# The router's sum: one-hots over nodes made by transposition instead of by comparison

## The chip, the core and the metric

The program runs on one core of one Trainium2 chip. The metric is the device time of one execution in microseconds (us), the median of several. A core has TensorE (PE; its weight loads are shown apart as PEld), VectorE (DVE), ScalarE (ACT), GpSimd (POOL) and SyncE (SP, which here only issues transfers). Each works through its own instructions in order; semaphores tie them together. L1985 means line 1985 of the kernel.

## What is computed

A graph block over 6250 nodes with 256 features: a graph transformer with two layers over 200,000 edges, a linear attention beside it, and a mixture of four experts, whose gates come from a graph attention router over 131,072 other edges. The change is in the router. Cut to that:

```python
h = (x_flat @ W_gat).reshape(M, HEADS, NUM_EXPERTS)      # 4 heads, 4 experts
src = concatenate([edge_index[0], loops]); dst = concatenate([edge_index[1], loops])
a_src = (h * att_src).sum(-1); a_dst = (h * att_dst).sum(-1)
e = leaky_relu(a_src[src] + a_dst[dst], 0.2)
e_max = segment_max(e, dst, num_segments=M)
ee = exp(e - e_max[dst])
denom = segment_sum(ee, dst, num_segments=M)
alpha = ee / (denom[dst] + 1e-16)
agg = segment_sum(h[src] * alpha[:, :, None], dst, num_segments=M)
```

## The kernel before

The program is a row of blocks, one after the other, with a barrier between: two edge lists are sorted by node tile, the two attention layers run over the first list, then the router over the second: `neighbour_max` (the maximum per node, with the experts beside it), `router_weights`, `neighbour_sum`, `gates`, and `answer`, which adds the experts' outputs to the result.

The change is in `neighbour_sum` alone. Nodes lie in 50 tiles of 125 (`NODE_TILE`). The sorted edges come in tiles of 128 lanes, two edge tiles (a pair) always belonging to one node tile. A step handles `WIDE` = 8 edge tiles, so 4 pairs; there are 141 steps, and all code is written out (`edge_steps`): in loop step n each engine runs its pieces in the order of its list, piece with lag l on edge step k = n + l. Buffers are picked by k modulo 2 or 4, and semaphores count steps.

Per step:

- SyncE (L1950) loads, for all partitions alike, the place of each of the 1024 edges in its node tile (`local`, 256 KB).
- VectorE, `near_hot` (L2060): compares `local` with the partition's number and gets `hot_t`, 125 nodes by 1024 edges, bf16, zeros and ones.
- TensorE, `fetch` (L2004): eight small matmuls with `hot_t` as weights take, for each edge, its destination's numbers from `node_info`; which tile is in a register, read eight at a time in every second step by `load_tiles` (L666, `TENSOR_LOAD`).
- VectorE, `gather_info` (L2049): sums the three bf16 parts into `info`.
- GpSimd, VectorE, ScalarE: `sums` (L1980), `leaky` (L2065), `less` (L1985), `exps` (L2027), `weigh` (L1963), and the split of the result into three bf16 parts: `high` (L2032), `rest_of` (L1970), `middle` (L2036), `low` (L1975).
- VectorE, `one_hot` (L2054): compares the numbers 0 to 124 (`node_no`, copied once to 8 x 125) with each edge's place (`g.loc`) and gets `hot`, 128 edges by 8 x 125 nodes, bf16. It holds the same ones as `hot_t`, the other way round.
- TensorE, `add_up` (L2015): eight matmuls with `hot` as weights sum the parts of the edges per node, two edge tiles into one piece of PSUM.
- VectorE, `add_sum(0..3)` (L2078): four additions of such a piece to `acc3` at the tile that a register tells. Each waits for the previous one, since two may meet the same tile.

The orders on the engines before:

```python
steps(pool, [(0, sums), (-1, less), (-2, weigh), (-3, rest_of), (-4, low)])
steps(pe, [(1, load_tiles), (-5, add_up), (1, fetch)])
steps(act, [(-3, high), (-4, middle), (-1, exps)])
steps(dve, [(0, gather_info), (-6, add_sum(0)), (-1, leaky), (-6, add_sum(1)), (2, near_hot), (-6, add_sum(2)),
            (-2, one_hot), (-6, add_sum(3)), (-6, load_tiles)])
```

Of the kernel before, what the change touches and what calls it, by code (L numbers as in the profile page):

```python
# [7 lines left out]
ALU = mybir.AluOpType  # L8
# [4 lines left out]
BF16 = mybir.dt.bfloat16  # L13
# [3 lines left out]
LANES = 128  # L17
PAIR = 2
NODE_TILE = 125
# [59 lines left out]
@contextmanager  # L79
def semaphores(nc, names):  # L80

    handles = [nc.alloc_semaphore(name=n) for n in names]
    yield handles
    nc.clear_and_free_semaphores(handles)
    nc.all_engine_barrier()


def sem_set(nc, ctx, prefix, names):
    handles = ctx.enter_context(semaphores(nc, [f"{prefix}_{n}" for n in names]))
    return dict(zip(names, handles))  # L90
# [491 lines left out]
def at(tensor, t):  # L582

    return tensor[:, t] if isinstance(t, int) else tensor[:, bass.ds(t, 1)].squeeze(1)
# [12 lines left out]
def wait(eng, sem, value):  # L597

    if not isinstance(value, int) or value > 0:
        eng.wait_ge(sem, value)  # L600
# [1304 lines left out]


WIDE = 8
SPLIT_SUMS = SPLIT * (FE + FH)


def neighbour_sum(nc, c, g, src_sb, node_info, gacc, ans):

    pairs = WIDE // PAIR
    with ExitStack() as st:
        def sb(n, shape, dt=F32):
            return st.enter_context(nc.sbuf_tensor(f"gs_{n}", shape, dt))

        def psum(n):
            return [st.enter_context(nc.psum_tensor(f"gs_{n}{h}", [LANES, 512], F32)) for h in range(2)]

        node_no = sb("node_no", [LANES, WIDE, NODE_TILE], BF16)
        hot = sb("hot", [LANES, 4, WIDE, NODE_TILE], BF16)
        local = sb("local", [LANES, 4, WIDE * LANES], BF16)
        hot_t = sb("hot_t", [NODE_TILE, 2, WIDE * LANES], BF16)
        info = sb("info", [LANES, 4, WIDE, 2 * FH])
        e_sb = sb("e_sb", [LANES, 4, WIDE, FH])
        vals = sb("vals", [LANES, 4, WIDE, FE + FH])
        rest = sb("rest", [LANES, 4, WIDE, FE + FH])
        parts = sb("parts", [LANES, 4, WIDE, SPLIT, FE + FH], BF16)
        acc3 = sb("acc3", [NODE_TILE, g.tiles, SPLIT_SUMS])  # L1930
        tile_of = sb("tile_of", [1, g.pairs], I32)
        ps_n, ps_sum = psum("ps_n"), psum("ps_sum")
        m = sem_set(nc, st, "gs", ["tiles_in", "cleared", "one_hots", "near_hots", "fetched", "info", "sums", "leaky",
                                   "less", "exps", "weighted", "high", "rest", "middle", "split", "summed", "added",
                                   "chain"])
        m["local_in"] = st.enter_context(semaphores(nc, [f"gs_local_in{j}" for j in range(4)]))
# [3 lines left out]
        def steps(eng, pieces):  # L1940
            edge_steps(eng, total, pieces)
# [47 lines left out]
        @block.tensor  # L1989
        def _(pe):  # L1990
            pe.wait_ge(m["tiles_in"], 16)

            numbers = TileNumbers(nc, pe, tile_of, g)

            def load_tiles(k, r, j):
                numbers.load((k + 1) * pairs)

            def fetch(k, r, j):
                pe.wait_ge(m["near_hots"], k + 1)
                wait(pe, m["info"], k - 1)  # L2000
                for p in range(pairs):
                    t = numbers.of(k * pairs + p)
                    for e in range(PAIR * p, PAIR * (p + 1)):
                        ins = pe.matmul(ps_n[j % 2][:, e * SPLIT * 2 * FH:(e + 1) * SPLIT * 2 * FH],  # L2004
                                        hot_t[:, j % 2, e * LANES:(e + 1) * LANES],
                                        at(node_info, t).rearrange("p n f -> p (n f)"), start=True, stop=True)
                ins.then_inc(m["fetched"], 1)

            def add_up(k, r, j):
                pe.wait_ge(m["split"], k + 1)  # L2010
                pe.wait_ge(m["one_hots"], k + 1)
                wait(pe, m["added"], pairs * (k - 2) + pairs)
                for p in range(pairs):
                    for e in range(PAIR):
                        ins = pe.matmul(ps_sum[j % 2][0:NODE_TILE, p * SPLIT_SUMS:(p + 1) * SPLIT_SUMS],  # L2015
                                        hot[:, k % 4, PAIR * p + e, :],
                                        parts[:, k % 4, PAIR * p + e].rearrange("p n f -> p (n f)"),
                                        start=e == 0, stop=e == PAIR - 1)
                ins.then_inc(m["summed"], 1)
            steps(pe, [(1, load_tiles), (-5, add_up), (1, fetch)])  # L2020

        @block.scalar
        def _(act):
            def exps(k, r, j):
                act.wait_ge(m["less"], k + 1)
                wait(act, m["split"], (k - 4) + 1)
                act.activation(vals[:, k % 4, :, FE:FE + FH], e_sb[:, k % 4], ACT.Exp).then_inc(m["exps"], 1)  # L2027

            def high(k, r, j):
                act.wait_ge(m["weighted"], k + 1)  # L2030
                wait(act, m["summed"], (k - 4) + 1)
                act.copy(parts[:, k % 4, :, 0, :], vals[:, k % 4]).then_inc(m["high"], 1)  # L2032

            def middle(k, r, j):
                act.wait_ge(m["rest"], k + 1)
                act.copy(parts[:, k % 4, :, 1, :], rest[:, k % 4]).then_inc(m["middle"], 1)  # L2036
            steps(act, [(-3, high), (-4, middle), (-1, exps)])

        @block.vector
        def _(dve):  # L2040
            chain = Chain(dve, m["chain"])
            dve.memset(acc3[:], 0.0)
            chain(dve.tensor_copy(node_no[:], c.node_no[:, 0:1, :].broadcast_to([LANES, WIDE, NODE_TILE])))
            dve.wait_ge(m["tiles_in"], 16)

            def gather_info(k, r, j):
                dve.wait_ge(m["fetched"], k + 1)
                wait(dve, m["less"], (k - 4) + 1)
                dve.tensor_reduce(info[:, k % 4], ps_n[j % 2][:, 0:WIDE * SPLIT * 2 * FH]  # L2049
                                  .rearrange("p (e n f) -> p e f n", e=WIDE, n=SPLIT), AX, ALU.add).then_inc(m["info"], 1)  # L2050

            def one_hot(k, r, j):
                wait(dve, m["summed"], (k - 4) + 1)
                dve.tensor_tensor(hot[:, k % 4], node_no[:], g.loc[:, bass.ds(k * WIDE, WIDE)].unsqueeze(2)  # L2054
                                  .broadcast_to([LANES, WIDE, NODE_TILE]), ALU.is_equal).then_inc(m["one_hots"], 1)

            def near_hot(k, r, j):
                dve.wait_ge(m["local_in"][j], (r + 1) * 16)
                wait(dve, m["fetched"], k - 1)
                dve.tensor_scalar(hot_t[:, j % 2, :], local[0:NODE_TILE, j], c.lane_no[0:NODE_TILE, :], None, ALU.is_equal)\  # L2060
                    .then_inc(m["near_hots"], 1)

            def leaky(k, r, j):
                dve.wait_ge(m["sums"], k + 1)
                dve.scalar_tensor_tensor(out=e_sb[:, k % 4], in0=e_sb[:, k % 4], scalar=0.2, in1=e_sb[:, k % 4],  # L2065
                                         op0=ALU.mult, op1=ALU.max).then_inc(m["leaky"], 1)

            numbers = TileNumbers(nc, dve, tile_of, g)

            def load_tiles(k, r, j):  # L2070
                numbers.load((k + 1) * pairs)

            def add_sum(p):
                def add(k, r, j):
                    t = numbers.of(k * pairs + p)
                    dve.wait_ge(m["summed"], k + 1)
                    wait(dve, m["added"], pairs * k + p)
                    dve.tensor_tensor(at(acc3, t), at(acc3, t), ps_sum[j % 2][0:NODE_TILE, p * SPLIT_SUMS:  # L2078
                                                                              (p + 1) * SPLIT_SUMS], ALU.add)\
                        .then_inc(m["added"], 1)  # L2080
                return add
            steps(dve, [(0, gather_info), (-6, add_sum(0)), (-1, leaky), (-6, add_sum(1)), (2, near_hot), (-6, add_sum(2)),
                        (-2, one_hot), (-6, add_sum(3)), (-6, load_tiles)])
            dve.wait_ge(m["added"], pairs * total)
            for n in range(SPLIT):
                chain(dve.tensor_tensor(gacc[:], gacc[:], acc3[:, :, n * (FE + FH):(n + 1) * (FE + FH)], ALU.add))
# [358 lines left out]
```

## Time and profile before

| what | value |
|---|---|
| median of 3 runs | 7925.82 us (7924.39 to 7932.85) |
| profiled execution | 7930.16 us, its span 7927.9 us |
| `neighbour_sum`, first L2060 to last L2078 | 7363.4 to 7781.3 us |
| L2054, one-hots over nodes | 141 of them, median 1187 ns |
| L2060, one-hots over edges | 141, median 637 ns |
| L2015 and L2004, matmuls | 1128 each |
| L2078, additions | 564, median 204 ns |
| after the router's sum: `gates` and `answer` | to 7927.9 us |

The span is that of the instructions the profiler saw, the execution's time includes a little around it. In a timeline a row is one instruction, or several alike that follow each other (xN); durations of neighbours on one engine may overlap, since the next one starts before the last is written, so the start-to-start distance tells what a piece costs its engine. Brackets at a row's end tell how long the engine stood idle and who released it.

### The profile page before, as it was taken

The page shows a single profiled execution, that of the slowest core. Times are in us where ns is not written, and L with a number is a line of the kernel's source. Part 1 is how long each engine was busy: PE and PEld are TensorE (multiplying, and loading weights), DVE is VectorE, ACT ScalarE, POOL GpSimd, SP SyncE. Part 2 cuts the span into 40 slices and gives each one's busy share as a digit, 9 for nine tenths or more (in the row PEclk, how much of TensorE's full clock was granted, in tenths as well). Part 3 has the DMA queues.
Part 4 walks back from the last instruction along what each step waited for, and adds up shares of the span by engine and source line. Part 5 has one row for each costly group of instructions (what it writes and reads, how often), then busy time and mean ns, then how long its engine had stood idle before and what let it go on. Part 6 is the DMA issues. An engine that isn't in the chain of part 4 may idle for free. (4 is left out here: it accounts for less than half of the span.)

```text
span 7927.9 us, 103405 instructions
## 1 busy us (share of the span) xinstructions
PE 5293.5 (67%) x27325; PEld 4204.5 (53%) x27325; DVE 5852.9 (74%) x15897; ACT 1022.4 (13%) x3273; POOL 5163.2 (65%) x5420
## 2 busy tenths in 40 slices
PE   5886855665665566556666666666559999999441
PEld 3553534555555555535555555555546666666331
DVE  7878845666666666667787878877766777777997
ACT  0000010000000000020000000000132222222230
POOL 2331306777777777737777777777617777777892
PEclk7555578778778877877887778878758888888555
DMA  1000034444444444434444444444432333332336
GB/s 31 3 3 8 3 95 125 129 128 129 128 129 128 128 129 130 128 97 126 126 127 126 125 125 126 126 125 126 125 82 52 63 62 57 62 63 55 114 96 179
DMA packets 504010, 776.97 MB, mean 98 GB/s; under 512 B 121545, under 2 KB 364222, under 8 KB 503442
## 3 DMA queue, kind: packets, MB, share of 16 engines
q0 software_dynamic: 202656, 454.22, 21.7%
q1 hardware_dynamic: 292838, 304.95, 14.7%
q10 hardware_dynamic: 7948, 11.21, 0.6%
q8 instruction: 237, 3.88, 0.2%
q14 instruction: 331, 2.71, 0.1%
HBM read 698.60 MB, written 71.36 MB: 97 GB/s over the span
## 5 line engine op out<-in xcount | busy, mean ns | idle before, releaser
L700 POOL DMA_INDIRECT att_kv_e<-kv,gnn_idx x3336 | 3366.1, 1009 | 1196.5 <-issue 1004.8
L773 PE MATMUL att_ps_sum<-att_vals,att_hot 128*125 128x136 f32 x6672 | 1345.1, 361 | 1638.6 <-DVE att_vals L822 1637.8
L773 PEld LDWEIGHTS att_ps_sum<-att_vals,att_hot 128*125 128x125 f32 x6672 | 1131.4, 246 | 1852.8 <-DVE att_vals L822 1845.7
L700 POOL DMA_INDIRECT max_rows<-rows,gat_idx x1128 | 1064.8, 944 | 568.3 <-issue 329.0
L798 DVE TENSOR_TENSOR att_prod<-att_ps_q,att_kv_e 128x512 f32<-128x512 f32 x834 | 575.9, 690 | 999.6 <-DMA att_kv_e<-kv,gnn_idx 633.5
L761 PE MATMUL att_ps_q<-qs,att_hot_t 125*128 x6672 | 1217.8, 344 | 26.9 <-DVE att_hot_t L811 26.9
L761 PEld LDWEIGHTS att_ps_q<-qs,att_hot_t 125*128 125x128 f32 x6672 | 1167.1, 262 | 28.1 <-issue 28.1
L1854 DVE CUSTOM_DVE_ANT_0 max_junk<-max_far,max_ps_b 125x256 bf16<-125x256 bf16 x2256 | 792.5, 416 | 259.2 <-PE max_ps_b L1818 256.1
L784 ACT ACTIVATE att_vals<-att_clipped 128x32 f32<-128x32 f32 x834 | 191.3, 229 | 4049.9 <-DVE att_clipped L830 4049.9
L838 DVE TENSOR_TENSOR acc<-acc,att_ps_sum 125x136 f32 x1668 | 484.4, 290 | 123.1 <-PE att_ps_sum L773 2.8
L822 DVE TENSOR_TENSOR att_vals<-att_kv_e,att_vals 128x512 f32<-128x512 f32 x834 | 567.6, 681 | 0.0
L817 DVE TENSOR_REDUCE att_dots<-att_prod 128x32 f32<-128x512 f32 x834 | 564.6, 677 | 0.1
L804 DVE TENSOR_TENSOR att_hot<-node_no,gnn_loc 128x500 f32<-128x500 f32 x834 | 558.4, 670 | 0.0
L2253 PE MATMUL ex_ps_o<-ex_w,ex_hid 128*125 128x256 f32 x1600 | 518.6, 480 | 0.0
L811 DVE TENSOR_SCALAR att_hot_t<-att_local,lane_no 125x512 f32<-125x512 bf16 x834 | 406.4, 487 | 42.3 <-DMA att_local<-gnn_loc_rows 42.3
L509 POOL DMA_INDIRECT gnn_table<-gnn_records,gnn_dest_sb x120 | 174.3, 1452 | 401.7 <-DVE gnn_records L425 372.2
L1818 PE MATMUL max_ps_b<-max_a_t,pick_head 12*125 12x512 bf16 x1128 | 375.6, 434 | 64.5 <-ACT max_a_t L1827 51.8
L2264 PE MATMUL ex_ps_h<-ex_xT,ex_w 128*128 128x250 f32 x1600 | 413.5, 404 | 0.0
L2253 PEld LDWEIGHTS ex_ps_o<-ex_w,ex_hid 128*125 128x125 f32 x1600 | 356.0, 234 | 89.4 <-issue 14.0
L480 PE MATMUL gnn_ps_perm<-gnn_moves,gnn_hot_low 125*128 125x96 f16 x1600 | 327.9, 387 | 81.6 <-DVE gnn_moves L430 81.6
L2264 PEld LDWEIGHTS ex_ps_h<-ex_xT,ex_w 128*128 128x128 f32 x1600 | 342.7, 214 | 57.9 <-issue 0.4
L480 PEld LDWEIGHTS gnn_ps_perm<-gnn_moves,gnn_hot_low 125*128 125x128 f16 x1600 | 235.2, 150 | 188.5 <-DVE gnn_moves L430 113.1
(445 smaller groups left out, 6887.5 us busy)
## 6 DMA issues: line engine op xcount, KB each, us to landing
att_local<-gnn_loc_rows SPq DMA_DIRECT2D x834, 128.0 KB
att_kv_e<-kv,gnn_idx POOLq DMA_INDIRECT x3336, 3.0
max_local<-gat_loc_rows SPq DMA_DIRECT2D x282, 128.0 KB
gs_local<-gat_loc_rows SPq DMA_DIRECT2D x141, 256.0 KB, 3.3
outs<-ex_y SPq DMA_DIRECT2D x25, 896.0 KB
max_rows<-rows,gat_idx POOLq DMA_INDIRECT x1128
ans_late<-outs SPq DMA_DIRECT2D x11, 896.0 KB
ans_early<-outs SPq DMA_DIRECT2D x8, 896.0 KB
```

The costliest lines, as they stand in the source:

```text
L480: ins = pe.matmul(ps_perm[k % 2][:, 0:2 * SLOTS_F], hot_low[:, k % 2, :, w], moves[:, k % 2, :, :, w], start=w == 0, stop=w == BLOCK - 1)
L700: pool.indirect_dma_start(rows(j, e), None, source, bass.IndirectOffsetOnAxis(ap=g.idx[:, t:t + 1], axis=0))\
L761: ins = pe.matmul(ps_q[j % 2][:, e * D:(e + 1) * D], hot_t[:, j % 2, e * LANES:(e + 1) * LANES], at(qs, t), start=True, stop=True)
L773: ins = pe.matmul(ps_sum[j % 2][0:NODE_TILE, p * 256:p * 256 + SUMS], hot[:, j, PAIR * p + e, :], vals[:, j % 2, PAIR * p + e, :], start=e ...
L798: dve.tensor_tensor(prod[:].rearrange("p (e d) -> p e d", e=GROUP), ps_q[j % 2][:, :].rearrange("p (e d) -> p e d", e=GROUP), kv_e[:, j, : ...
L804: dve.tensor_tensor(hot[:, j], c.node_no[:], own_tile(g, k), ALU.is_equal)\
L817: dve.tensor_reduce(dots_sb[:, j % 2, :], prod[:].rearrange("p (h d) -> p h d", d=HEAD), AX, ALU.add).then_inc(m["dots"], 1)
L822: dve.tensor_tensor(vals[:, j % 2, :, 0:D].rearrange("p e (h d) -> p e h d", d=HEAD), kv_e[:, j, :, D:2 * D].rearrange("p e (h d) -> p e h ...
L838: dve.tensor_tensor(a, a, ps_sum[j % 2][0:NODE_TILE, p * 256:p * 256 + SUMS], ALU.add)\
L1854: ins = dve.tensor_tensor_reduce(out=junk[:, j % 2, 2 * n + i, :], in0=far[:, j % 2, i * 256:(i + 1) * 256], in1=ps_b[n][0:NODE_TILE, i * ...
L2253: ins = pe.matmul(self.ps_o[0:NODE_TILE, 0:GIN], self.hid[:, e % 2, hc, k * NODE_TILE:(k + 1) * NODE_TILE], self.w2[:, e, hc, :], start=hc ...
L2264: ins = pe.matmul(self.ps_h[:, i * TWO:(i + 1) * TWO].rearrange("p (t n) -> p t n", t=2), self.w1[:, e, ch, a:a + LANES], self.xT[:, s % 2 ...
```

## The change

`one_hot` leaves VectorE. TensorE turns `hot_t` by eight transposes (`turn`, 128 x 125 each, with the identity as the moving operand) into a new pair of PSUM buffers `ps_hot`, and ScalarE copies them to `hot` (`one_hot`, 128 x 1000). `hot` has six buffers (`HOTS`) instead of four, since it is now filled with lag 0 instead of -2. `near_hot` waits for the transposes of two steps before, where it waited for their fetch; the transposes wait for the copy of two steps before. `node_no` in bf16 and its setup copy go.

```diff
+HOTS = 6
-        node_no = sb("node_no", [LANES, WIDE, NODE_TILE], BF16)
-        hot = sb("hot", [LANES, 4, WIDE, NODE_TILE], BF16)
+        hot = sb("hot", [LANES, HOTS, WIDE, NODE_TILE], BF16)
+        ps_hot = [st.enter_context(nc.psum_tensor(f"gs_ps_hot{h}", [LANES, WIDE, LANES], BF16)) for h in range(2)]
...
+            def turn(k, r, j):
+                pe.wait_ge(m["near_hots"], k + 1)
+                wait(pe, m["one_hots"], k - 1)
+                for e in range(WIDE):
+                    ins = pe.transpose(ps_hot[j % 2][:, e, 0:NODE_TILE], hot_t[:, j % 2, e * LANES:(e + 1) * LANES],
+                                       c.ident16[0:NODE_TILE, 0:NODE_TILE])
+                ins.then_inc(m["turned"], 1)
...
-                                        hot[:, k % 4, PAIR * p + e, :],
+                                        hot[:, k % HOTS, PAIR * p + e, :],
...
-            steps(pe, [(1, load_tiles), (-5, add_up), (1, fetch)])
+            steps(pe, [(1, load_tiles), (-5, add_up), (1, fetch), (1, turn)])
...
-            steps(act, [(-3, high), (-4, middle), (-1, exps)])
+
+            def one_hot(k, r, j):
+                act.wait_ge(m["turned"], k + 1)
+                wait(act, m["summed"], (k - HOTS) + 1)
+                act.copy(hot[:, k % HOTS], ps_hot[j % 2][:, :, 0:NODE_TILE]).then_inc(m["one_hots"], 1)
+            steps(act, [(-3, high), (-4, middle), (-1, exps), (0, one_hot)])
...
-            dve.memset(acc3[:], 0.0)
-            chain(dve.tensor_copy(node_no[:], c.node_no[:, 0:1, :].broadcast_to([LANES, WIDE, NODE_TILE])))
+            chain(dve.memset(acc3[:], 0.0))
...
-            def one_hot(k, r, j):
-                wait(dve, m["summed"], (k - 4) + 1)
-                dve.tensor_tensor(hot[:, k % 4], node_no[:], g.loc[:, bass.ds(k * WIDE, WIDE)].unsqueeze(2)
-                                  .broadcast_to([LANES, WIDE, NODE_TILE]), ALU.is_equal).then_inc(m["one_hots"], 1)
...
-                wait(dve, m["fetched"], k - 1)
+                wait(dve, m["turned"], k - 1)
...
-                        (-2, one_hot), (-6, add_sum(3)), (-6, load_tiles)])
+                        (-6, add_sum(3)), (-6, load_tiles)])
```

VectorE's instructions in the middle of the stage, in a step with a load of tile numbers, before (ISA is the arithmetic on the register that holds the tile; gs_acc is `acc3`):

```order
17609 L2060 TENSOR_SCALAR gs_hot_t<-gs_local,lane_no 125x1024
17610 L2078 ISA
17611 L2078 TENSOR_TENSOR gs_acc<-gs_acc,gs_ps_sum 125x60
17612 L2054 TENSOR_TENSOR gs_hot<-gs_node_no,gat_loc 128x1000
17613 L2078 ISA
17614 L2078 TENSOR_TENSOR gs_acc<-gs_acc,gs_ps_sum 125x60
17615 L666 TENSOR_LOAD gs_tile_of
17616 L2049 TENSOR_REDUCE gs_info<-gs_ps_n 128x64
```

The same place on VectorE in the changed kernel (L2068, L2086 and L2062 are the old L2060, L2078 and L2049):

```order
17549 L2068 TENSOR_SCALAR gs_hot_t<-gs_local,lane_no 125x1024
17550 L2086 ISA
17551 L2086 TENSOR_TENSOR gs_acc<-gs_acc,gs_ps_sum 125x60
17552 L2086 ISA
17553 L2086 TENSOR_TENSOR gs_acc<-gs_acc,gs_ps_sum 125x60
17554 L666 TENSOR_LOAD gs_tile_of
17555 L2062 TENSOR_REDUCE gs_info<-gs_ps_n 128x64
```

The one-hot between the third and the fourth addition is gone, and the two are neighbours, ahead of the load.

TensorE at a step's end and the next one's start before, again where a load stands (the last row begins the next fetch):

```order
6991 L2004 ISA
6992 L2004 MATMUL gs_ps_n<-node_info,gs_hot_t 128x24 x2
6993 L666 TENSOR_LOAD gs_tile_of
6994 L2015 MATMUL gs_ps_sum<-gs_parts,gs_hot 125x60 x8
6995 L2004 ISA
```

And in the changed kernel (L2005 and L2024 are the old L2004 and L2015):

```order
7089 L2005 ISA
7090 L2005 MATMUL gs_ps_n<-node_info,gs_hot_t 128x24 x2
7091 L2014 MATMUL gs_ps_hot<-ident,gs_hot_t 128x125 x8
7092 L666 TENSOR_LOAD gs_tile_of
7093 L2024 MATMUL gs_ps_sum<-gs_parts,gs_hot 125x60 x8
7094 L2005 ISA
```

Eight transposes now stand between the fetch and the load of tile numbers.

## Rows read from the trace of the kernel before

**Rows 1.** Windows: the stage; busy us (xcount) by engine, PEclk, DMA share, GB/s.

```profile
7363.40:7776.50 413.10, 179.16 (x2247) 164.37 (x2248) 407.17 (x1117) 123.79 (x423) 408.32 (x705) 0.50 0.34 101
```

**Rows 2.** Timeline, one step on VectorE: start us, us, engine, line, operation.

```profile
7559.80 0.34 DVE L2049 TENSOR_REDUCE gs_info<-gs_ps_n 128x64 f32<-128x192 f32 x1
7560.09 0.22 DVE L2078 TENSOR_TENSOR gs_acc<-gs_acc,gs_ps_sum 125x60 f32 x1
7560.22 0.51 DVE L2065 SCALAR_TENSOR_TENSOR gs_e_sb<-gs_e_sb 128x32 f32<-128x32 f32 x1
7560.66 0.20 DVE L2078 TENSOR_TENSOR gs_acc<-gs_acc,gs_ps_sum 125x60 f32 x1
7560.78 0.64 DVE L2060 TENSOR_SCALAR gs_hot_t<-gs_local,lane_no 125x1024 bf16<-125x1024 bf16 x1
7561.34 0.20 DVE L2078 TENSOR_TENSOR gs_acc<-gs_acc,gs_ps_sum 125x60 f32 x1
7561.47 1.19 DVE L2054 TENSOR_TENSOR gs_hot<-gs_node_no,gat_loc 128x1000 bf16<-128x1000 bf16 x1
7562.58 0.20 DVE L2078 TENSOR_TENSOR gs_acc<-gs_acc,gs_ps_sum 125x60 f32 x1
7562.71 0.34 DVE L2049 TENSOR_REDUCE gs_info<-gs_ps_n 128x64 f32<-128x192 f32 x1
```

**Rows 3.** Timeline, GpSimd in the same step.

```profile
7559.82 0.41 POOL L1963 TENSOR_TENSOR gs_vals<-src_sb,gs_vals 128x128 f32<-128x128 f32 x1
7560.19 0.49 POOL L1970 TENSOR_TENSOR gs_rest<-gs_vals,gs_parts 128x160 f32<-128x160 f32 x1
7560.65 0.49 POOL L1975 TENSOR_TENSOR gs_parts<-gs_rest,gs_parts 128x160 bf16<-128x160 f32 x1
7561.10 0.43 POOL L1980 TENSOR_TENSOR gs_e_sb<-src_sb,gs_info 128x32 f32<-128x32 f32 x1
7561.49 1.27 POOL L1985 TENSOR_TENSOR gs_e_sb<-gs_e_sb,gs_info 128x32 f32<-128x32 f32 x1
7562.73 0.41 POOL L1963 TENSOR_TENSOR gs_vals<-src_sb,gs_vals 128x128 f32<-128x128 f32 x1
```

**Rows 4.** Single lines over the stage: shortest, median and longest ns.

```profile
L2060 DVE TENSOR_SCALAR gs_hot_t<-gs_local,lane_no x141: 474/637/766, 7363.4 to 7761.4; 125x1024 bf16<-125x1024 bf16 x141
...
L2065 DVE SCALAR_TENSOR_TENSOR gs_e_sb<-gs_e_sb x141: 176/511/515, 7366.2 to 7769.0; 128x32 f32<-128x32 f32 x141
```

**Rows 5.** Timeline, GpSimd in the stage's fill, without one-hots beside it.

```profile
7367.29 0.25 POOL L1985 TENSOR_TENSOR gs_e_sb<-gs_e_sb,gs_info 128x32 f32<-128x32 f32 x1
7367.50 0.41 POOL L1963 TENSOR_TENSOR gs_vals<-src_sb,gs_vals 128x128 f32<-128x128 f32 x1
```

**Rows 6.** Timeline, VectorE's adds side by side in the drain; the load's line.

```profile
7775.42 0.22 DVE L2078 TENSOR_TENSOR gs_acc<-gs_acc,gs_ps_sum 125x60 f32 x1 [0.21 <-DVE gs_acc L2078]
7776.26 0.22 DVE L2078 TENSOR_TENSOR gs_acc<-gs_acc,gs_ps_sum 125x60 f32 x1 [0.62 <-PE gs_ps_sum L2015]
7776.69 0.22 DVE L2078 TENSOR_TENSOR gs_acc<-gs_acc,gs_ps_sum 125x60 f32 x1 [0.21 <-DVE gs_acc L2078]
...
L666 DVEq TENSOR_LOAD <-gs_tile_of x71: 344/596/600, 7362.8 to 7779.3; - x71
```

**Rows 7.** TensorE: timeline of one step, four transposes of the stage before, f32 ones.

```profile
7561.19 1.06 PE L2015 MATMUL gs_ps_sum<-gs_parts,gs_hot 128*125 128x60 bf16 x8 [1.65 <-POOL gs_parts L1975]
7562.06 0.39 PE L2004 MATMUL gs_ps_n<-node_info,gs_hot_t 125*128 x8
...
7343.98 0.59 PE L1809 MATMUL max_ps_a<-ident,max_rows 128*12 128x128 bf16 x4 [1.61 <-DMA max_rows<-rows,gat_idx]
...
L1374 PE MATMUL enter_ps_t<-ident,enter_xn x100: 267/271/438, 1060.9 to 1208.3; 125*128 125x125 f32 x100
```

**Rows 8.** ScalarE: a cast from SBUF, a copy from PSUM.

```profile
L2032 ACT CAST gs_parts<-gs_vals x141: 324/324/327, 7367.9 to 7772.8; 128x160 bf16<-128x160 f32 x141
...
L1827 ACT COPY max_a_t<-max_ps_a x282: 574/574/577, 5911.8 to 7344.6; 12x512 bf16<-12x512 bf16 x141
```

More of the change, by code:

```diff
@@ L1932, in neighbour_sum @@
         ps_n, ps_sum = psum("ps_n"), psum("ps_sum")
-        m = sem_set(nc, st, "gs", ["tiles_in", "cleared", "one_hots", "near_hots", "fetched", "info", "sums", "leaky",
+        ps_hot = [st.enter_context(nc.psum_tensor(f"gs_ps_hot{h}", [LANES, WIDE, LANES], BF16)) for h in range(2)]
+        m = sem_set(nc, st, "gs", ["tiles_in", "cleared", "turned", "one_hots", "near_hots", "fetched", "info", "sums", "leaky",
                                    "less", "exps", "weighted", "high", "rest", "middle", "split", "summed", "added",
```

## The prediction

> **What bounds the kernel now.** I read the windows first, to find the stretch, then the timeline of one step there engine by engine, then single lines for the shortest and the usual duration of the same instruction.
>
> The change lies in the router's sum, 141 steps between 7363.4 and 7781.4 us. Over it VectorE is busy 407.2 of 413.1 us and GpSimd 408.3, TensorE 179.2 at a granted clock of 0.50 (the 1.2 GHz level), ScalarE 123.8 [rows 1]. Nothing else runs there, so what a step gets shorter the kernel gets shorter. A step is 2.91 us from one L2049 to the next [rows 2].
>
> Two engines look full. GpSimd's fullness is partly waiting: its last subtraction, L1985, takes 1.27 us in the steady part, exactly alongside VectorE's one-hot L2054 [rows 2, 3], and 0.25 us in the fill, where no one-hot stands beside it [rows 5]. Its own pace is 0.21 for L1985 [rows 5] and as much for L1980 of the same size, 0.37 for L1963, 0.46 and 0.45 for the two casts that follow [rows 3]: 1.70 us. L1980 is held 0.18 longer (0.39 to the next start) while L2060 runs, L1985 1.03 longer (1.24). 1.70 + 0.18 + 1.03 = 2.91, the step. So GpSimd is only full because VectorE locks it out; it does the same to VectorE on a smaller scale: L2060 needs 474 ns at best and usually 637, L2065 176 at best and usually 511 [rows 4].
>
> VectorE's step by starts [rows 2]: L2049 0.29, add 0.13, L2065 0.44, add 0.12, L2060 0.56, add 0.13, one-hot L2054 1.11, add 0.13. It is the bound, and the one-hot is its largest piece.
>
> **The change on VectorE.** The one-hot goes: its 1.11 and the 0.13 that the add before it took, 1.24 us of every step. Two things stood in its cover and now show.
>
> First, the third and fourth add stand side by side, and each add waits for the one before it to be complete. In the drain, adds side by side start 0.43 us apart (7776.26 to 7776.69) [rows 6]. So 1.24 goes and 0.43 comes: 2.91 - 1.24 + 0.43 = 2.10 us.
>
> Second, the load of the next eight tile numbers (L666). It stands after the fourth add of every second step and takes VectorE's sequencer 596 ns [rows 6]. Before, the sequencer does it while the engine is in the 1.19 us one-hot, and in the step shown, which has one, the fourth add to L2049 still takes 0.13 [rows 2]. Now what is ahead of it is a wait that the sequencer can't pass until the third add is done, so it begins with only the 0.2 us fourth add as cover. The drain shows this very order: add, load, next piece: 0.84 us from 7775.42 to 7776.26 against 0.43 without a load [rows 6]. Taking 0.84 in place of 0.13 in every second step: 2.10 and 2.81, mean 2.46.
>
> Third, a credit. The waits for GpSimd are inside this: 637 - 474 = 0.16 us of L2060, and of L2065's only what exceeds the 0.43 that its neighbouring adds need anyway (0.13 + 0.44 - 0.43 = 0.14): 0.30 a step. GpSimd's 1.70 of 2.91 us become 1.70 of some 2.4, but it can catch up during each load. With all the waits gone a step would be 2.16, with none gone 2.46. I take a third gone, nearer to the row as it stands because GpSimd still has work in most of the step: 2.35 us.
>
> The setup copy of the node numbers goes too: 1000 elements, no more than a one-hot, so under 1 us once; I take 1. The wait of L2060 is now for the transposes instead of the fetch. That is under 1 us later in the same step of TensorE, one step ahead of L2060's own; I cost it at nothing, its cover being the 0.84 us of L2049, two adds and L2065 that VectorE does first. The wait would hold up both last adds and the next L2049, which all stand behind it.
>
> **On TensorE.** Eight transposes of 125 columns a step are new. Now the eight sums of a step start 0.87 us before the fetches, so 0.109 apart, at the 1.2 GHz level, and the fetches take 0.39 [rows 7]. No transposition of a 125x128 bf16 tile is in the trace. From below: spacing as of the sums, 8 x 0.109 = 0.87. From above, if pipelined: four bf16 transposes of 128 columns take 0.59 [rows 7], 0.148 each, 1.18. TensorE is then 2.13 to 2.44 us a step, less the end of a run that the next covers. I take the lower end: the shape of the load and the column count are nearest to the sums'. That is under 2.35, so it costs nothing; at the upper end it would be level with VectorE, and at most 0.1 us more. TensorE's own load of tile numbers (the same 0.6 us) now stands behind the transposes, which are queued work that covers it.
>
> **On ScalarE.** One copy of 1000 elements from PSUM. From 324 ns for 160 elements and 574 for 512 [rows 8] comes 0.71 ns an element, 574 + 488 x 0.71 = 0.92 us. With the two casts and the exponential (32 elements, at most a cast's) 0.92 + 3 x 0.32 = 1.9 us: under 2.35, though no longer idle. Behind the copy in ScalarE's order stands the next step's L2032, for which GpSimd's L1970 waits; L1970 is fourth of five there, over 1 us into GpSimd's step, and that hides it.
>
> **GpSimd** gets 1.70 plus its wait for L2060, 0.2 to 0.3: 2.0 us, under 2.35. The broadcast loads come at 2.35 instead of 2.91 us; the DMA engines' share of 0.34 [rows 1] becomes 0.42, with four buffers.
>
> **Sum.** 141 x (2.905 - 2.35) = 78, + 1 = 79 us. The profiled execution took 7930.2 (span 7927.9), the median of the runs is 7925.8; the saving is the same off either: 7925.8 - 79 = 7847.
>
> **Rivals.**
> (a) The load stays hidden, because the sequencer gets far enough ahead during L2060. Then a step is 2.10 or a little less, until TensorE at 2.0 to 2.13 binds: 141 x 0.80 + 1 = 114, 7812. Against: the wait of the fourth add can't be passed [rows 6].
> (b) The waits for GpSimd grow instead: its three long instructions are 0.4 to 0.5 us each [rows 3], and L2060 may come right behind the start of one. Doubled waits give 2.16 + 0.60 = 2.76, 7905. Both waits at a whole instruction (2.16 + 0.45 + 0.30) give 2.91: no change.
> (c) Slower: the transposes run one by one. The own duration of one is 271 ns for a tile of this shape in f32 [rows 7]. TensorE's present 1.26 us (from the first sum to the last fetch's end [rows 7]) plus 8 x 0.271 = 3.43: 141 x 0.52 = 74 us slower, less 1, 7999. It decides from 0.206 us each, (2.905 - 1.26)/8. For it: three engines now take turns on TensorE's results. Against it: the four of L1809 take 0.59 together, 0.148 each.
> The Trainium skill (TensorE: Matmul & The Clock Gate, Part 4: PE-mode transpose) gives about 275 ns for a 128x128 bf16 transpose in a kernel, most of it access latency. Paid by each in a row, it would speak against the whole change: 1.26 + 8 x 0.275 = 3.46 us a step, 8003 us. The trace has four of them overlapping, so I hold it for a latency; no run so far shows eight.
> (d) The change doesn't remove a bound, GpSimd's 1.27 us being its own: 7926. Against it [rows 5].
>
> **How the numbers follow.** Forecast (2.16 to 2.6 us a step, 7820 to 7884) 0.68; (a) 0.14; (b) at 7905 0.07; (b) full or (d), no change, 0.04; (c) 0.07. The range runs from 7808, which takes in (a) but for its fastest end, to 7884: some 0.8. A measurement of this kernel can tell about 0.2%, 16 us, from no change. Faster 0.68 + 0.14 + 0.07 = 0.89, same 0.04, slower 0.07.
>
> **What would show it.** No L2054; adds in VectorE's timeline 0.43 apart at the step's end; L2049 0.13 after the fourth add in one step and 0.84 in the next, so steps that alternate by 0.7; L1985 near 0.25 instead of 1.27; eight transposes in about 0.9 to 1.2 us; one ScalarE copy of about 0.92. I am wrong if L2049 is found waiting for fetches or L2060 for transposes (TensorE binds), if L2060 or L2065 have grown beyond 637 and 511, or if steps don't alternate.

## The result, and the profile after

The changed kernel takes 7854.5 us (median of 4 runs, 7845.2 to 7857.5), the kernel before 7925.1: a ratio of 0.9908, interval 0.9890 to 0.9925, so 71 us less. Two further comparisons (below) gave 76 us (7929.5 to 7853.4) and 74 (9080.1 to 9006.5). The prediction was 7847.

The windows of 100 us in the middle of the router's sum, in the columns of [rows 1]:

```profile
7400.00:7500.00 100.00, 87.98 (x1015) 77.86 (x1012) 74.20 (x296) 65.66 (x169) 82.33 (x211) 0.50 0.51 142
```

VectorE, full in [rows 1], is busy 74 of 100 us, GpSimd 82, TensorE 88 and ScalarE 66, still at the granted clock of 0.50. No engine is full by this measure, yet nothing but the step's own order limits it. Two steps on VectorE show how, in the columns of [rows 2]:

```profile
7560.13 0.35 DVE L2062 TENSOR_REDUCE gs_info<-gs_ps_n 128x64 f32<-128x192 f32 x1
7560.42 0.22 DVE L2086 TENSOR_TENSOR gs_acc<-gs_acc,gs_ps_sum 125x60 f32 x1
7560.56 0.18 DVE L2073 SCALAR_TENSOR_TENSOR gs_e_sb<-gs_e_sb 128x32 f32<-128x32 f32 x1
7560.85 0.22 DVE L2086 TENSOR_TENSOR gs_acc<-gs_acc,gs_ps_sum 125x60 f32 x1
7560.98 0.74 DVE L2068 TENSOR_SCALAR gs_hot_t<-gs_local,lane_no 125x1024 bf16<-125x1024 bf16 x1
7561.65 0.20 DVE L2086 TENSOR_TENSOR gs_acc<-gs_acc,gs_ps_sum 125x60 f32 x1
7562.06 0.22 DVE L2086 TENSOR_TENSOR gs_acc<-gs_acc,gs_ps_sum 125x60 f32 x1 [0.21 <-DVE gs_acc L2086]
7562.80 0.36 DVE L2062 TENSOR_REDUCE gs_info<-gs_ps_n 128x64 f32<-128x192 f32 x1 [0.52 <-issue]
...
7564.70 0.22 DVE L2086 TENSOR_TENSOR gs_acc<-gs_acc,gs_ps_sum 125x60 f32 x1 [0.21 <-DVE gs_acc L2086]
7564.83 0.35 DVE L2062 TENSOR_REDUCE gs_info<-gs_ps_n 128x64 f32<-128x192 f32 x1
```

The first step runs from 7560.13 to 7562.80, 2.67 us, the second to 7564.83, 2.03. They differ behind the fourth add: 0.74 us to L2062 where the load of tile numbers stands (the row's "issue": the engine waits for nothing but its own sequencer), 0.13 where none does. The mean is 2.35 us, against 2.91 in [rows 2].

TensorE, ScalarE and GpSimd in the second of these steps, and single lines of the whole stage (shortest, median and longest ns, as in [rows 4]):

```profile
7563.69 1.00 PE L2014 MATMUL gs_ps_hot<-ident,gs_hot_t 125*128 125x125 bf16 x8
7563.88 0.97 ACT L2050 COPY gs_hot<-gs_ps_hot 128x1000 bf16<-128x1000 bf16 x1
7563.67 0.41 POOL L1964 TENSOR_TENSOR gs_vals<-src_sb,gs_vals 128x128 f32<-128x128 f32 x1
7564.04 0.68 POOL L1971 TENSOR_TENSOR gs_rest<-gs_vals,gs_parts 128x160 f32<-128x160 f32 x1
...
L2068 DVE TENSOR_SCALAR gs_hot_t<-gs_local,lane_no x141: 478/740/820, 7360.9 to 7686.5; 125x1024 bf16<-125x1024 bf16 x141
L2073 DVE SCALAR_TENSOR_TENSOR gs_e_sb<-gs_e_sb x141: 175/184/325, 7363.8 to 7692.2; 128x32 f32<-128x32 f32 x141
L2014 PE MATMUL gs_ps_hot<-ident,gs_hot_t x1128: 215/310/314, 7362.0 to 7689.9; 125*128 125x125 bf16 x188
L1986 POOL TENSOR_TENSOR gs_e_sb<-gs_e_sb,gs_info x141: 244/252/255, 7364.2 to 7692.4; 128x32 f32<-128x32 f32 x141
```

L1986 is the old L1985, 1.27 us in [rows 3]: 0.25 throughout. L2073, the old L2065, has lost its wait (511 ns in [rows 4], now 184). L2068, the old L2060, waits longer (637, now 740). GpSimd pays for this meeting too: its L1971, which starts before L2068 is done, takes 0.68 us where the old L1970 took 0.49 [rows 3]; that costs nothing, since GpSimd then waits for VectorE. From the first to the last of the 141 L2068 it is 325.6 us; [rows 4] gives 398.0 for L2060, so 72 us lie there. Another 3 lie in the drain (19.9 us from the last L2060 to the stage's end before, 16.9 now) and 0.5 in the setup.

### The profile page after: what moved, and what is told of

The parts are those of the page before. It is cut to its first block and busy times, and to the rows that moved or that the text cites. A ratio compares the mean times of both kernels' runs of the same rounds, so it can differ in the third digit from the quotient of the medians.

```text
span 7849.7 us, 105934 instructions
## 1 busy us (share of the span) xinstructions
PE 5432.2 (69%) x28453; PEld 4324.3 (55%) x28453; DVE 5691.3 (73%) x15755; ACT 1119.2 (14%) x3414; POOL 5033.1 (64%) x5420
```

## The experiments

The measure that is most exact is the time from the first to the last of the 141 edge one-hots (L2060, here mostly L2068), since it leaves out everything else. It is 398.0 us before and 325.6 after; two more profiles of the changed kernel give 321.3 and 321.5. The runs below were made on three chips. On one the kernel before took 7929.5 us, on the other two 9080.0 and 9080.1: there the attention layers and the neighbours' maximum ran about 1.1 ms longer, and why is open; the router's sum is the same (321.5 against 321.3). So every time below is given beside the kernel before on the same chip. The changed kernel itself was run on the first (7853.4) and on one of the other two (9006.5, 74 us less than before). The runs beside 9080.0 are from the third chip, without the changed kernel: there only savings can be compared, and the time between the edge one-hots is the better measure.

**The changed kernel again**, on two chips, as the base for the others.

> The changed kernel unaltered, on the chip of this call, as the base for the others. All theories: 70 to 78 us below the kernel before on the same chip, steps of 2.04 and 2.67 us.

Measured: 7853.4 beside 7929.5, ratio 0.9902 (0.9886 to 0.9919). On another chip:

> The changed kernel unaltered, on the chip of this call, as the base: 70 to 78 us below the kernel before, steps of 2.04 and 2.67 us.

Measured: 9006.5 beside 9080.1, ratio 0.9914 (0.9898 to 0.9931). As expected.

**VectorE's part alone.** The kernel before, without any one-hots over nodes (TensorE's wait for them goes too):

```diff
             steps(dve, [(0, gather_info), ..., (2, near_hot), (-6, add_sum(2)),
-                        (-2, one_hot), (-6, add_sum(3)), (-6, load_tiles)])
+                        (-6, add_sum(3)), (-6, load_tiles)])
```

> The kernel before without the one-hots over nodes: hot is filled with zeros once, and neither TensorE nor ScalarE makes them instead, so the sums are wrong. It prices VectorE's part of the change alone. Theory (TensorE's transposes and ScalarE's copy are hidden): the same step pattern as the changed kernel, 2.0 and 2.65 us, mean within 0.05 of 2.35, time within 10 us of 7854. Rival (the added work costs something): faster than the changed kernel by 20 us or more.

Measured: 9004.3 beside 9080.0, ratio 0.9920 (0.9898 to 0.9941), 76 us less; 321.4 us from the first to the last edge one-hot, where the changed kernel has 321.5. The two kinds of step are there without a transpose in sight:

```profile
8702.20 0.22 DVE L2078 TENSOR_TENSOR gs_acc<-gs_acc,gs_ps_sum 125x60 f32 x1 [0.21 <-DVE gs_acc L2078]
8702.93 0.36 DVE L2049 TENSOR_REDUCE gs_info<-gs_ps_n 128x64 f32<-128x192 f32 x1 [0.52 <-issue]
...
8704.84 0.22 DVE L2078 TENSOR_TENSOR gs_acc<-gs_acc,gs_ps_sum 125x60 f32 x1 [0.21 <-DVE gs_acc L2078]
8704.98 0.35 DVE L2049 TENSOR_REDUCE gs_info<-gs_ps_n 128x64 f32<-128x192 f32 x1
```

So the transposes and the copy cost nothing that this measure shows; the whole gain, and what is missing from it, is VectorE's.

**Half of the added work.** The changed kernel with `range(WIDE // 2)` transposes and a copy of that half.

> The changed kernel with four transposes a step instead of eight and a copy of half the width; the other half of hot is zeros, so the sums are wrong. It takes 0.44 us off TensorE and 0.4 off ScalarE. Theory (VectorE's order sets the step): within 8 us of 7854. Rival (TensorE's or ScalarE's load, or a chain through them, sets it): 30 to 60 us faster.

Measured: 9008.1 beside 9080.0, ratio 0.9911 (0.9886 to 0.9935), 72 us less, and 323.6 us between the edge one-hots, no fewer than the changed kernel's 321.3 to 325.6. Neither TensorE's nor ScalarE's load sets the step.

**Twice the transposes.**

```diff
-                for e in range(WIDE):
+                for e in list(range(WIDE)) * 2:
```

> The changed kernel with every transpose done twice (sixteen a step, same results). TensorE's step grows by 8 spacings of 0.10 us from about 1.93 to 2.75 us. Theory (transposes are pipelined, TensorE has 0.42 us a step to spare): TensorE becomes the bound at 2.75 to 2.9, the kernel 55 to 75 us slower than the changed one. Rival (c) of the prediction (each transpose costs its own 0.3 us where the queue is full): a step of 4.3 us, 270 us slower. If TensorE had over 0.8 us to spare: no change.

Measured: 7855.6 beside 7929.5, ratio 0.9909 (0.9892 to 0.9926), where the changed kernel had 0.9902, and 322.8 us between the edge one-hots: nothing, and that was not expected. The windows tell why (columns as above):

```profile
7500.00:7600.00 100.00, 80.38 (x1376) 73.94 (x1376) 74.33 (x300) 66.69 (x172) 83.71 (x215) 0.93 0.40 120
```

With sixteen transposes the granted clock is mostly at the 2.4 GHz level (0.91 to 0.93 in windows of 80 to 100 us from 7400 on); with eight it was 0.50. TensorE does a third more instructions in less busy time (80 of 100 us against 88). It is not one profile alone: the mean clock of the whole execution is 0.757 to 0.764 in the four runs with sixteen and 0.740 to 0.744 in those with eight. So adding transposes raised the clock here. Now and then it is at 0.50 for a few us, and a timeline of TensorE has both prices of sixteen transposes (the granted clock is 1.00 from 7515 to 7520 us and 0.50 from 7562.20 to 7563.90):

```profile
7516.86 1.04 PE L2014 MATMUL gs_ps_hot<-ident,gs_hot_t 125*128 125x125 bf16 x16
...
7562.26 1.84 PE L2014 MATMUL gs_ps_hot<-ident,gs_hot_t 125*128 125x125 bf16 x16
```

At 0.50 the extra eight cost 0.84 us (1.84 against 1.00), as the expectation had it, and with them TensorE has no pause in that step; at 1.00 all sixteen cost about what eight cost at 0.50. The expectation failed on the clock and not on the transposes, and a whole stage with sixteen at the 1.2 GHz level was not seen. Either price rules out the prediction's rival (c), which would need 4.3 us a step.

The Trainium skill (TensorE: Matmul & The Clock Gate, Part 4: PE-mode transpose) says that a transpose "doesn't count as PE-busy the same way" and that the full clock does not engage for it; this run, which adds nothing but transposes and is granted 0.93 in place of 0.50, does not agree.

**The load of tile numbers, moved under the edge one-hot.** In the changed kernel:

```diff
-            steps(dve, [(0, gather_info), (-6, add_sum(0)), (-1, leaky), (-6, add_sum(1)), (2, near_hot), (-6, add_sum(2)),
-                        (-6, add_sum(3)), (-6, load_tiles)])
+            steps(dve, [(0, gather_info), (-6, add_sum(0)), (-1, leaky), (-6, add_sum(1)), (2, near_hot), (-6, load_tiles),
+                        (-6, add_sum(2)), (-6, add_sum(3))])
```

> The changed kernel, with VectorE's load of tile numbers moved from behind the fourth add to right behind the edge one-hot (near_hot), whose 0.74 us stand in the engine while the sequencer loads. Theory (VectorE's own order sets the step): the steps with a load shrink from 2.67 us by 0.45 to 0.6, since the third add may come 0.2 later than now; steps 2.05 to 2.25, stage and kernel 30 to 42 us shorter than the changed kernel. Rival (TensorE's 2.1 us of work with its waits sets the step): no gain, 7854. Third possibility: the gain stops at TensorE's 2.07 us a step.

Measured: 8978.3 beside 9080.0, ratio 0.9889 (0.9870 to 0.9909), 102 us less, about 28 more than the changed kernel saved (74). Between the edge one-hots it is 304.1 us, only 17 less than 321.5; the other 11 us are within the spread of the runs. Both are below the 30 to 42 us expected: a step with a load shrinks by 0.4 us and not by 0.45 to 0.6, and late broadcasts take back part (5.9 us in five waits, 0.9 in the changed kernel's profile with 321.5). Steps are 2.07 and 2.24 us:

```profile
8699.72 0.74 DVE L2068 TENSOR_SCALAR gs_hot_t<-gs_local,lane_no 125x1024 bf16<-125x1024 bf16 x1
8700.53 0.22 DVE L2086 TENSOR_TENSOR gs_acc<-gs_acc,gs_ps_sum 125x60 f32 x1
8700.96 0.22 DVE L2086 TENSOR_TENSOR gs_acc<-gs_acc,gs_ps_sum 125x60 f32 x1 [0.21 <-DVE gs_acc L2086]
8701.10 0.35 DVE L2062 TENSOR_REDUCE gs_info<-gs_ps_n 128x64 f32<-128x192 f32 x1
...
8701.95 0.73 DVE L2068 TENSOR_SCALAR gs_hot_t<-gs_local,lane_no 125x1024 bf16<-125x1024 bf16 x1
8702.61 0.20 DVE L2086 TENSOR_TENSOR gs_acc<-gs_acc,gs_ps_sum 125x60 f32 x1
```

The first edge one-hot has the load behind it: the next add comes 0.81 us later instead of 0.66, and that is all that still shows of the load's 0.6 us. The uncovered load is the cause of the alternation.

**The same move in the kernel before.**

> The kernel before, with the same move of the load (behind near_hot, ahead of the third add and the one-hot). Theory: the load was hidden behind the one-hot, so nothing is gained; it may lose up to 0.2 us in every second step (0 to 14 us) where it now delays the third add. Rival (the load costs VectorE wherever it stands): 30 to 40 us faster as in the first run.

Measured: 9099.6 beside 9080.0, ratio 1.0029 (1.0016 to 1.0041), 20 us slower; 420.7 us between the edge one-hots. That the load was hidden before is confirmed: nothing is gained. But the loss is more than the 14 us expected, because steps without a load became longer too. The same trace has both patterns. Early in the stage (8530 to 8545 us) steps alternate between 3.22 and 2.61 us, a mean of 2.91 as before the move; then comes one of 3.66 us, and from there on most take 3.05 us. GpSimd and VectorE have locked into another phase, that is, other instructions of theirs now start together:

```profile
8700.41 0.74 DVE L2060 TENSOR_SCALAR gs_hot_t<-gs_local,lane_no 125x1024 bf16<-125x1024 bf16 x1
8700.46 0.42 POOL L1963 TENSOR_TENSOR gs_vals<-src_sb,gs_vals 128x128 f32<-128x128 f32 x1
8700.83 0.67 POOL L1970 TENSOR_TENSOR gs_rest<-gs_vals,gs_parts 128x160 f32<-128x160 f32 x1
8701.08 0.20 DVE L2078 TENSOR_TENSOR gs_acc<-gs_acc,gs_ps_sum 125x60 f32 x1
8701.20 1.36 DVE L2054 TENSOR_TENSOR gs_hot<-gs_node_no,gat_loc 128x1000 bf16<-128x1000 bf16 x1
8701.47 1.45 POOL L1975 TENSOR_TENSOR gs_parts<-gs_rest,gs_parts 128x160 bf16<-128x160 f32 x1
```

The one-hot L2054 itself now waits (1.36 us, 1.19 in [rows 2]), and it holds up L1975 instead of L1985 (1.45 us, 0.49 in [rows 3]). Who waits for whom is a matter of phase, and moving one piece moves it.

**Is it GpSimd that the edge one-hot waits for?** The changed kernel, with GpSimd's product L1964 over two of the eight edge tiles (and `vals` set to zero once, ahead of the loop):

```diff
-                pool.tensor_tensor(vals[:, k % 4, :, 0:FE]...
+                pool.tensor_tensor(vals[:, k % 4, 0:2, 0:FE]...
```

> The changed kernel with GpSimd's product L1964 over two of the eight edge tiles only (the other products stay zero, so the sums are wrong): 128x32 elements, about 0.25 us instead of 0.41. Nothing on VectorE, TensorE or ScalarE changes in the loop. Theory (the edge one-hot, 740 ns against 478 at best, waits until GpSimd's L1964 is off the memory port they share): it drops to 570 to 620 ns and both kinds of step shrink by 0.12 to 0.17, 17 to 24 us. Rival A (the 740 ns are its own here): no change. Rival B (it is caught by the next GpSimd instruction instead): 740 or more, no gain.

Measured: 8989.2 beside 9080.1, ratio 0.9894 (0.9877 to 0.9910), 17 us less than the changed kernel on that chip (9006.5); 304.2 us between the edge one-hots against 321.5. Its lines:

```profile
L2070 DVE TENSOR_SCALAR gs_hot_t<-gs_local,lane_no x141: 478/569/697, 8534.2 to 8838.4; 125x1024 bf16<-125x1024 bf16 x141
...
L1964 POOL TENSOR_TENSOR gs_vals<-src_sb,gs_vals x141: 234/243/535, 8538.8 to 8845.5; 128x32 f32<-128x32 f32 x141
```

L1964 is 0.17 us shorter (0.41 to 0.24), and the edge one-hot, in which nothing was changed, is 0.17 shorter too (740 to 569). Both kinds of step are 0.17 us shorter as well (2.64 and 2.07 us to 2.47 and 1.90, from one edge one-hot to the next). Rivals A and B fall: what holds the edge one-hot up is GpSimd's instruction that started with it.
The Trainium skill (GPSIMD Engine Reference, 1. Specifications) says that GpSimd's memory interfaces are shared with VectorE and contended by VectorE's instructions with two SBUF inputs or in a 2-port mode; that fits L1985, which is held up by L2054 with its two SBUF inputs. L2068 has one input, and no trace here shows in which mode it ran, nor that an interface is what the two share.

**Smaller loads, and more buffers.** On top of the early load, VectorE reads four numbers in each step instead of eight in every second:

```diff
-            numbers = TileNumbers(nc, dve, tile_of, g)
+            numbers = TileNumbers(nc, dve, tile_of, g, pairs)
```

> As e1_load_early, and VectorE reads four tile numbers in every step instead of eight in every second: about 0.34 us of its sequencer instead of 0.6, which fits under the edge one-hot. Theory: all steps 2.05 to 2.1 us, 40 to 48 us below the changed kernel and 10 to 14 below the early load of eight (which gave 2.07 and 2.24). Rival (TensorE's 1.93 us of work plus its waits bind at about 2.15): no gain over the early load of eight.

Measured: 7819.8 beside 7929.5, ratio 0.9861 (0.9844 to 0.9877), 34 us below the changed kernel (7853.4). Most steps are 2.07 us, whether they have a load or not, and the alternation is gone. About one in eight takes 2.2 to 2.4 us, and three are much longer: 5.90, 3.32 and 2.95 us from one edge one-hot to the next. In all it is 294.0 us between the edge one-hots, 27 less than the changed kernel's 321.3; the 40 to 48 us expected did not come. Then six buffers for `local` instead of four:

> As e6_small_loads, with six buffers for the broadcast edge places instead of four. In the changed kernel one step near the first early load of the answer took 3.56 us (in the early-load kernel three or four of 2.9 to 4.6). Theory (the edge places land late behind that transfer, and four shorter steps cover less of it): these stalls go, 3 to 8 us less than e6_small_loads. Rival (the stalls are something else): the same time as e6_small_loads.

Measured: 7819.6 beside 7929.5, ratio 0.9862 (0.9846 to 0.9879). Between the edge one-hots it is 288.4 us, 5.6 less: the three long steps are gone, and the waits (us in all, times, longest) say why, first with four buffers, then with six:

```profile
DVE gs_hot_t L2068 <- DMA gs_local<-gat_loc_rows: 6.2, 4, 3.8
```

```profile
DVE gs_hot_t L2068 <- DMA gs_local<-gat_loc_rows: 1.1, 2, 0.6
```

The profile shows the gain, the medians don't (0.3 us); with runs that spread over 8 and 13 us that stays open. Both versions beat both kernels.

**What bounds that version.** TensorE is busy 98 of 100 us in it. The same with half the transposes:

> The kernel e7_six_locals (all steps 2.07 us, TensorE 98% busy at the 1.2 GHz level) with four transposes a step and half the copy; the other half of hot is zeros, so the sums are wrong. Theory (VectorE's order sets 2.07 here too): steps stay at 2.05 to 2.07, time as e7_six_locals, 107 to 112 us below the kernel before. Rival (TensorE's 2.0 us of work is by now the bound): steps shrink below 2.03 and the time by 6 us or more beyond that.

Measured: 8982.1 beside 9080.1, ratio 0.9886 (0.9869 to 0.9903), 98 us less where 107 to 112 were expected; the interval (88 to 119 us) takes that in. Between the edge one-hots it is 288.1 us against 288.4. The step is the same, so TensorE does not bind even there: at 2.07 us it is still VectorE's order.

## Why the prediction was right

- **What bounds.** VectorE's own order, with GpSimd full only because VectorE holds it up: right. L1985 came down to 252 ns, and VectorE's part alone gives the same 321 us.
- **Adds side by side**, 0.43 us where the one-hot's 1.24 had been: measured 0.41 (7561.65 to 7562.06).
- **The load without cover**, 0.84 us in place of 0.13 in every second step: measured 0.74 (7562.06 to 7562.80), shown by moving it. It is the term that a count of busy time would have missed: 0.3 us a step, over a third of the 0.83 that is left of 1.24 once the adds stand side by side. Its size came from a row that doesn't show it: the add at 7776.26 [rows 6] ends a wait of 0.62 us for TensorE's sums (`<-PE gs_ps_sum L2015`), so 0.84 was the price of that wait. That it came near 0.74 was luck.
- **The credit for fewer waits** was mis-sized, and by luck it did no harm. I took 0.10 off the 0.30 us a step. In the trace L2065's wait is gone whole (0.14 of effect), while that of the edge one-hot has grown from 0.16 to 0.26 (740 - 478): 0.04 in all. The step is 2.35 all the same, since the load shows 0.10 us less than I took in every second step (0.05 a step) and the adds 0.02 less. The reason given, that GpSimd has more slack, holds for the one; for the other the phase decides: each step L2068 now starts just as GpSimd starts L1964 and ends 0.28 us after it. The quarter-width run shows that pairing. L2068 beyond 637 ns was named as a sign of being wrong, and it came: this part of the mechanism was wrong, the rest was not.
- **TensorE.** Eight transposes take 1.00 us and start 0.10 apart ((1.00 - 0.31) / 7), below the 0.109 that I took from the sums: they are pipelined, that is, each starts before the one ahead is done. Each by itself takes 310 ns, longer than the 271 that rival (c) charged, so the duration of one would have misled; the row of four in 0.59 us [rows 7] was the one to go by. TensorE's step of 2.13 was a little high: 2.07 us are enough, as the six-buffer kernel shows. L2068's new wait for the transposes, taken at nothing, was 1.5 us in all, in four steps at the stage's start.
- **ScalarE**: 0.97 us measured for 0.92 forecast, hidden as forecast.
- **The transfers** I took at no cost for four buffers. In one profile of the changed kernel one step took 3.55 us (L2062 at 7390.15 to 7393.70) and its edge one-hot waited 1.7 us for its broadcast; in the faster versions such waits reached 6.2 us in all. The median landing of 3.3 us is well covered by four steps of 2.35, but the longest, 10.3 us, is not. The wait comes about 12 us after an early load of the answer is issued; that this load causes it was not tested.
- **The sum**: 79 us forecast, 71 to 76 measured. Between the edge one-hots 141 x 0.555 was to give 78, and 72 to 77 came. I counted all 141 steps alike, but the first six were short already before, while VectorE's order was not yet full: they gained 2 us (10.6 to 8.6) and not 3.3. The late broadcast took 1.7 more in the profile with 72. The setup copy, taken at 1 us, gave 0.5 (3.77 us from the stage's memset to the first edge one-hot, now 3.25, where a broadcast is waited for instead), and 3 us in the drain had not been counted.
- **Rivals.** (a), the hidden load, falls with the alternation; (b) came true in part, for one of the two waits, by 0.10 us; (c) falls with 1.00 us for eight; (d) with L1986's 252 ns.

## What to carry to other kernels

When an instruction leaves a full engine, count what stood in its shadow: here 1.24 us left and 0.72 came back, 0.31 of it a register load that the one-hot had hidden, and 0.41 a wait between two additions that it had kept apart. Both can be looked for elsewhere in the trace, where the same order stands in a drain or a fill; but read the bracket of such a row before its distance is used: the drain's adds did show the 0.43, while the row taken for the load showed a wait for TensorE. After such a change reorder the rest: moving one load and halving it gave another 34 us, and in the kernel before the move alone lost 20.

## What the runs showed of the hardware that was not expected

- Sixteen transposes a step instead of eight took the granted clock from 0.50 to 0.93 and cost no time. In the six-buffer version TensorE was busy 98 of 100 us and stayed at 0.50; with sixteen transposes it was busy 80 and was granted 0.93. Sixteen transposes took 1.84 us at 0.50 and 1.04 at 1.00.
- VectorE's edge one-hot and GpSimd's product start within 0.05 us of each other, and the one-hot ends 0.28 us after the product, 0.29 when the product is shorter: 0.17 us less in one is 0.17 less in the other.
- In the kernel before, a move that touched a load in every second step lengthened most steps, with a load or without, from 2.91 to 3.05 us, since the two engines settled in another phase.
- A load of eight tile numbers takes 0.596 us of VectorE's sequencer, one of four 0.346.
- Two chips took 1.1 ms longer than a third in the attention layers and the neighbours' maximum, and not at all longer in this stage.
